# Branch input from scaled streams, bias products between the M products, and accumulating DMAs for the mix, in a four-layer attention and feed-forward kernel

## The reference, cut to what matters

```python
H_res = sinkhorn_log(x_norm @ W_res.T + H_res_base)   # per token 4x4, 50 row and 50 column normalisations
H_pre, H_post = softmax(...), softmax(...)             # per token 4 weights each
H_res = (1.0 - g) * I + g * H_res
x_pre = einsum('btnc,btn->btc', x_streams, H_pre)      # 4 streams of 256 columns -> 256
y = x_pre @ W_branch                                   # 256 x 256
x_mixed = einsum('btij,btjc->btic', H_res, x_streams)  # 16 products of 256 columns for each token
return x_mixed + einsum('btc,btn->btnc', y, H_post)
```

## Time and profile before

| what | value |
|---|---|
| median of 3 runs | 1242.49 us |
| profiled execution, its own time | 1239.2 us |
| its span | 1237.4 us |
| TensorE busy | 1180.8 us (95%) |
| VectorE busy | 798.3 us (65%) |
| ScalarE busy | 475.6 us (38%) |
| GpSimd busy | 101.4 us (8%) |
| mean granted clock of TensorE | 0.982 |

### The profile page before, as it was taken

The page is one execution under the profiler, slowest core; times in us unless marked ns, Lnnn a source line. Parts: engine busy times, 40 slices in busy tenths (PEclk is TensorE's granted clock), DMA queues, the critical chain, the costliest instruction groups (busy, mean ns, idle before and its releaser), DMA issues.

```text
span 1237.4 us, 16474 instructions
## 1 busy us (share of the span) xinstructions
PE 1180.8 (95%) x6458; PEld 588.8 (48%) x6458; DVE 798.3 (65%) x1556; ACT 475.6 (38%) x716; POOL 101.4 (8%) x80
## 2 busy tenths in 40 slices
PE   3989999988999999999999999999999999999998
PEld 2434665553454445454444444444444444444444
DVE  7685898989998246887776767767767652222220
ACT  7784353583235223534434334434343231111110
POOL 4410020025101310020000000000001000000000
PEclk8888899998999999999999999999999999999999
DMA  9630000014103214120121121111110231111310
GB/s 370 210 112 1 2 2 1 1 69 137 34 14 107 64 29 143 68 103 12 57 69 65 38 69 35 67 69 34 68 52 24 66 139 47 46 46 47 118 43 22
DMA packets 26061, 83.57 MB, mean 68 GB/s; under 512 B 3648, under 2 KB 4288, under 8 KB 25984
## 3 DMA queue, kind: packets, MB, share of 16 engines
q1 hardware_dynamic: 25984, 82.53, 19.7%
HBM read 76.22 MB, written 6.29 MB: 67 GB/s over the span
## 4 chain that ended last, share of the span: by engine, by line
PE 80%; DVE 12%; ACT 4%; issue 2%; DMA 1%; ACTq 0%; SPq 0%; DVEq 0%
PE PAIR L2221 31%; PE PAIR L1870 12%; PE PAIR L1871 12%; PE PAIR L1872 12%; DVE LORA L1268 3%; PE PAIR L1935 2%; PE PAIR L2178 1%; PE PAIR L1967 1%; DVE LORA L1267 1%; PE PAIR L2033 1%; DVE LORA L1266 1%; PE PAIR L1952 1%; PE PAIR L2058 1%; PE PAIR L2233 1%; ACT POOL L596 1%
## 5 line engine op out<-in xcount | busy, mean ns | idle before, releaser
L1870 PE MATMUL PAIR<-POOL 128*128 128x512 f16 x688 | 261.9, 381 | 3.9 <-DVE POOL L1349 3.0
L1871 PE MATMUL PAIR<-POOL 128*128 128x512 f16 x688 | 261.6, 380 | 0.0
L1872 PE MATMUL PAIR<-POOL 128*128 128x512 f16 x688 | 261.4, 380 | 0.0
L2221 PE MATMUL PAIR<-XT,POOL 128*128 128x512 f16 (+1 forms) x1056 | 239.0, 379 | 1.0 <-ACT ST L842 1.0
L2221 PEld LDWEIGHTS PAIR<-XT,POOL 128*128 128x128 f16 (+1 forms) x1056 | 102.6, 98 | 120.5 <-issue 2.5
L2221 PE MATMUL PAIR<-X,POOL 128*128 128x512 f16 (+1 forms) x528 | 121.2, 379 | 0.0
L1870 PEld LDWEIGHTS PAIR<-POOL 128*128 128x128 f16 x688 | 67.3, 98 | 84.6 <-issue 5.3
L1872 PEld LDWEIGHTS PAIR<-POOL 128*128 128x128 f16 x688 | 67.4, 98 | 81.9 <-issue 1.1
L1871 PEld LDWEIGHTS PAIR<-POOL 128*128 128x128 f16 x688 | 67.5, 98 | 74.2 <-issue 0.8
L1485 DVE SCALAR_TENSOR_TENSOR STG<-STG,PAIR 128x1024 f32<-128x1024 f32 (+2 forms) x32 | 28.1, 884 | 92.7 <-PE PAIR L2233 89.1
L876 ACT ACTIVATE POOL<-STG 128x1024 f16<-128x1024 f32 (+2 forms) x32 | 25.0, 788 | 145.5 <-DVE STG L1485 145.5
(11 more groups left out here) (280 smaller groups left out, 1656.4 us busy)
## 6 DMA issues: line engine op xcount, KB each, us to landing
STG<-in_gate_w SPq DMA_DIRECT2D x21, 512.0 KB, 3.5
STG<-in_up_w SPq DMA_DIRECT2D x21, 512.0 KB, 4.3
STG<-in_ctx_t SPq DMA_DIRECT2D x16, 512.0 KB, 4.2
STG<-in_ctx SPq DMA_DIRECT2D x16, 512.0 KB, 4.4
STG<-in_down_w SPq DMA_DIRECT2D x16, 512.0 KB, 3.5
POOL<-in_ctx SPq DMA_DIRECT2D x12, 512.0 KB, 11.0
X<-in_x SPq DMA_DIRECT2D x8, 512.0 KB, 9.7
out_t<-X SPq DMA_DIRECT2D x16, 256.0 KB, 2.9
```

The source lines that it names most:

```text
L1870: e.matmul(dst, l_hi, r_hi, start=first, stop=False)
L1871: e.matmul(dst, l_hi, r_lo, start=False, stop=False)
L1872: return e.matmul(dst, l_lo, r_hi, start=False, stop=last)
L2221: i = e.matmul(dst, blk[:, a_, k, :], src[:, b_, k, :], start=(opens and k == 0 and n == 0), stop=(k == KD // 2 - 1 and n == 2), skip_grou ...
```

## The change

- `bias_products` goes. Its matmuls stand inside `m_half`, two of 2 columns after each group of three 512-column matmuls, 256 as before; `bias_raw` (ScalarE) and `bias_terms` (VectorE) move behind M and behind the mix of batch 1. `row_sums` (TensorE) moves ahead of `logit_product(1)` and `row_terms` (VectorE) ahead of the logits.
- The branch input: ScalarE scales the four streams of `H` (`branch_streams`, 4 x 128x256), GpSimd adds them up in three operations of 128x256 (`branch_sum`), and TensorE only transposes the result (2 transposes).
- `add_share` is an accumulating DMA from GpSimd's queue, each after the one before; tile g of batch 1 is issued after `branch_sum(g + 4)`.
- Batch 2's mix: VectorE does streams 0 and 1 of tiles 4 to 7, ScalarE scales streams 2 and 3 into 1024-column buffers (`mix_help(4)` to `(7)`, two pairs of buffers used in turn), and 8 accumulating DMAs add them (`add_help`), one at a time.
- 30 joint Sinkhorn steps and 69 for each batch alone, in portions of 1, 27, 11, 11, 11, 6, 2 where they were 1, 25, 11, 11, 11, 5; `bias_terms` stands between `norm_ask(2, 4)` and `norm_rest(2, 4)`, ahead of the first of them.
- GpSimd's `context_lo` is four operations of 256 columns instead of one of 1024.
- PSUM pairs change: `MIX_PAIR` 3, 1 to 1, 0 and `T3_PAIR` 0, 2, 3, 1 to 2, 3, 1, 0; `third_transpose(0)` waits for the last `m_lo`, `third_transpose(1)` for `braw_ok`.

```diff
-JOINT = 35
+JOINT = 30
@@ GpSimd
+            def branch_sum(g):
+                b_, half = BS[g % 2], D // 2
+                e.wait_ge(bs_ok, g + 1)
...
+                e.tensor_tensor(b_[:, 0:CST], b_[:, 0:CST], b_[:, half:half + CST], ALU.add)
+                e.tensor_tensor(b_[:, CST:half], b_[:, CST:half], b_[:, half + CST:D], ALU.add).then_inc(p_step, 1)
+                e.wait_ge(p_step, 6 + g)
+                e.tensor_tensor(XB[g % 2], b_[:, 0:CST], b_[:, CST:2 * CST], ALU.add).then_inc(bx_ok, 1)
             def add_share(g):
                 e.wait_ge(py_ok, g + 1)
-                e.tensor_tensor(X[:, g, :], X[:, g, :], SHARE[g], ALU.add).then_inc(share_ok, 1)
+                if g:
+                    e.wait_ge(summed, 16 * g)
+                e.dma_start(X[:, g, :], SHARE[g], accum_op=ALU.add).then_inc(summed, 16)
+            def add_help(g):
+                for n in range(2):
+                    e.wait_ge(mixed, g + 1)
+                    e.wait_ge(help_ok, 2 * (g - 2) + n + 1)
+                    e.wait_ge(summed, 16 * (NT + 2 * (g - BT) + n))
+                    e.dma_start(X[:, g, :], XT1M[2 * (g % 2) + n], accum_op=ALU.add).then_inc(summed, 16)
@@ GpSimd, context_lo
-                e.tensor_tensor(lo, STAGE[n % SLOTS], hi, ALU.subtract).then_inc(c_lo, 1)
+                for q in range(0, D, CST):
+                    last = e.tensor_tensor(tile[:, 1, q:q + CST], STAGE[n % SLOTS][:, q:q + CST], tile[:, 0, q:q + CST],
+                                           ALU.subtract)
+                last.then_inc(c_lo, 1)
@@ GpSimd, order
-            for g in range(BT):
-                add_share(g)
+            for g in range(NT):
+                branch_sum(g)
+                if 4 <= g:
+                    add_share(g - 4)
...
+            for g in range(BT, NT):
+                add_help(g)
@@ ScalarE
-                    i = e.activation(DG[g % 2][:, n, :], IDF[:, :], ACT.Copy, scale=PRE[:, NST * g + n:NST * g + n + 1])
+                    i = e.activation(BS[g % 2][:, n * CST:(n + 1) * CST], H[:, g, n * CST:(n + 1) * CST], ACT.Copy,
+                                     scale=PRE[:, NST * g + n:NST * g + n + 1])
@@ ScalarE, mix_help
+                if g >= BT:
+                    e.wait_ge(summed, 16 * (NT + max(0, 2 * (g - BT - 1))))
@@ ScalarE, order
             exponential(0)
+            mix_help(4)
+            mix_help(5)
             weights_hi(0)
             exponential(1)
+            mix_help(6)
+            mix_help(7)
             weights_hi(1)
             exponential(2)
@@ VectorE, order
+            bias_terms()
+            norm_rest(2, 4)
             second_steps(0, 1)
-            norm_rest(2, 4)
             done = 1
-            for n, more in enumerate((25, 11, 11, 11, 5)):
+            for n, more in enumerate((27, 11, 11, 11, 6, 2)):
...
+                elif n == KD // 2:
+                    maximum(0)
@@ TensorE, m_half
                 for d in range(KD):
                     last = m_step(i, d, h)
+                    for s_ in range(2):
+                        bias = e.matmul(PAIR[3][:, at:at + 2], W2[2 * d + h][:, s_, i * P:(i + 1) * P],
+                                        BQ16[:, d, 2 - 2 * h:4 - 2 * h], start=False, stop=(d == KD - 1 and s_ == 1),
+                                        skip_group_check=True)
@@ TensorE, branch_in
-                    for n in range(NST):
-                        at = n * CST + k * P
-                        i = e.matmul(PAIR[3][:, k * P:(k + 1) * P], H[:, g, at:at + P], DG[g % 2][:, n, :],
-                                     start=(n == 0), stop=(n == NST - 1))
+                    i = e.transpose(PAIR[3][:, k * P:(k + 1) * P], XB[g % 2][:, k * P:(k + 1) * P], IDF[:, :])
```

More of the change, by code:

```diff
@@ L289, in build @@
                              "lgt_ok", "lg_raw"))
[L290 to L291 removed]
+        w_hi, m_hi, m_lo, braw_ok, sink_a, soft_a, bs_ok, xp_ok, y_ok, py_ok, help_ok, mdg_ok = (
+            sem(n) for n in ("w_hi", "m_hi", "m_lo", "braw_ok", "sink_a", "soft_a", "bs_ok", "xp_ok", "y_ok",
                              "py_ok", "help_ok", "mdg_ok"))
@@ L997, in _ @@
             m_lo_of(KD - 1)
+            bias_raw()
             third_normal(1)
@@ L1302, in weight_lo, with mix @@
                                        ALU.subtract).then_inc(w_lo, 1)
[L1304 to L1311, removed]
+            def mix(g):
+                sj1 = 1 if 2 <= g < BT else 2
+                e.wait_ge(summed, 16 * (g + 1))
+                for sj in range(sj1):
                     for si in range(NST):
@@ L1315, in mix @@
                                                    xs, ALU.mult, ALU.add)
-                    chain(i)
+                    if g < BT or sj + 1 < sj1:
+                        chain(i)
+                if g >= BT:
+                    i.then_inc(mixed, 1)
             def mix_end(g):
@@ L1669, in _ @@
             mix_factors(1)
-            mix(4, 0, 2)
-            maximum(0)
-            mix(4, 2, 4)
+            mix(4)
             weights_sum(0)
-            stats_of(4)
-            mix(5, 0, 2)
+            mix(5)
+            mix(6)
             maximum(1)
             weights_lo(0)
-            mix(5, 2, 4)
+            mix(7)
+            mixed_stats(4)
             weights_sum(1)
-            stats_of(5)
-            mix(6, 0, 2)
+            mixed_stats(5)
+            weights_lo(1)
             maximum(2)
-            weights_lo(1)
-            mix(6, 2, 4)
             weights_sum(2)
+            mixed_stats(6)
             maximum(3)
@@ L1692, in _ @@
             weights_sum(3)
-            stats_of(6)
-            mix(7)
-            stats_of(7)
+            mixed_stats(7)
             norm_ask(4, 8)
@@ L1987, in m_half @@
                     e.wait_ge(ctx_ok, 1)
+                    e.wait_ge(bq_ok, 1)
+                    e.wait_ge(tmp_ok, 1)
+                    e.wait_ge(lg_raw, B)
+                    e.matmul(PAIR[3][:, HALF + 64:HALF + 65], ONESF[:, :], col(TMP), start=True, stop=True)
                 elif i in (1, 2) and h == 0:
@@ L2038, in branch_product @@
                 e.wait_ge(xp_ok, g + 1)
-                if g:
-                    e.wait_ge(y_ok, g)
-                else:
+                if g == 0:
                     e.wait_ge(wb_in, 16)
                 for k in range(2):
-                    i = e.matmul(PAIR[3][:, HALF:HALF + CST], XPT[g % 2][:, k, :], WBF[:, k, :], start=(k == 0),
+                    i = e.matmul(PAIR[3][:, CST:2 * CST], XPT[g % 2][:, k, :], WBF[:, k, :], start=(k == 0),
                                  stop=(k == 1))
@@ L2064, in third_transpose @@
                 e.wait_ge(n3_ok, g + 1)
-                if g < 2:
-                    e.wait_ge(m_lo, KD - 1 + g)
+                if g == 0:
+                    e.wait_ge(m_lo, KD)
+                elif g == 1:
+                    e.wait_ge(y_ok, NT)
+                    e.wait_ge(braw_ok, 1)
                 if g >= BT:
```

110 lines of the change are left out of this document (48 added, 62 removed).

## The result

The changed kernel takes 1251.28 us (median of 4 runs, 1249.9 to 1251.96), the kernel before 1242.44 on the same chip: ratio 1.0078, 95% interval 1.0059 to 1.0097. It is slower by 0.8%, where 1232.0 was forecast.

What follows compares the result with a forecast made beforehand. TensorE was four fifths of the wait chain, with VectorE's Sinkhorn chain late up to 260 us and at 290 to 333. Gains 5.5 + 9.4 + 0.95 - 5.3 = 10.5 us gave 1228.7, as median 1232.0; range 1224 to 1241.

Steps and rivals of the forecast that it cites:

- quarters of 0.53 us now meet some 22 steps; at 0.25 us each they make VectorE 5.5 us slower there: Projections and score(0): GpSimd's quarters slow VectorE's Sinkhorn steps by 5.5 us, bringing back about 2.2 us of new waits.
- the three waits, 8.6 us, go: Projections, 290 to 321 us: TensorE's three waits for VectorE's lo halves vanish, as batch 2's 28 steps finish earlier.
- Rival 3: Quarters don't help, Sinkhorn scalings lose as much as before: gain about 1 to 3 us, 1240 us; chance 0.13.
- Factors of batch 1: VectorE's Sinkhorn chain beside M: the factors come 5.4 us earlier, at 225.6 instead of 230.9.
- M's end, 226: TensorE's building of M starts near 125.2 and ends near 226 instead of 241.6, saving 15 us.
- rival 4: TensorE's 15 us saved at M come through: gain near 20 us, 1222 us; chance 0.04.
- The first projection, 262.5: Behind the factors of batch 1, all VectorE's: the first projection moves 5.5 us earlier, from 268.0 to 262.5.
- Accumulations, L = 5.2: Batch 2's mix: time from one accumulating DMA's issue to the next is 5.2 us, kept open from 3.5 to 11.
- rival 1: Accumulations are quick, L under 3.9, with no wait on ScalarE: gain 15.9 us, 1226.6 us; chance 0.24.
- rival 2: Accumulations are slow: gain used up at L = 7.0, 1250 us at L = 8, half clock returns; chance 0.12.
- The wait for the third exponential: After score(3), TensorE waits 5.3 us for exponential(2), which follows mix_help(7) and four accumulations on ScalarE.
- The sum: Whole kernel: 5.5 + 9.4 + 0.95 - 5.3 = 10.5 us off the profiled execution.

Runs made afterwards that it cites:

- run 1: Changed kernel with GpSimd's context_lo as one operation of 1024 columns again: 1249.16 us, ratio 1.0061.
- run 4: Changed kernel with context_lo in two operations of 512 columns: 1248.67 us, ratio 1.0061.
- run 5: Changed kernel with GpSimd waiting for the landing of the accumulating DMAs of add_share(6) and add_share(7), quarters back to back: 1244.03 us, ratio 1.0021.
- run 7: Changed kernel with a wait for the first quarter only of context_lo(0) and context_lo(2), behind two DMAs: 1238.12 us, ratio 0.9969.
- run 2: Kernel before with only context_lo changed, to four operations of 256 columns, no DMA issued by GpSimd there: 1238.18 us, ratio 0.9969.
- run 6: Changed kernel with batch 2's four shares added by GpSimd instructions again instead of DMAs: 1247.19 us, ratio 1.0049.
- run 3: Changed kernel with GpSimd waiting for each quarter of context_lo to end before starting the next: 1238.9 us, ratio 0.9975.
- run 11: Run 8 with the 256 bias matmuls in one piece ahead of M instead of between M's products: 1230.66 us, ratio 0.9907.
- run 9: Changed kernel with the edits of run 7 and run 8 together, without waits between all quarters: 1235.25 us, ratio 0.9953.
- run 10: Run 3 with batch 2's mix wholly on VectorE, no add_help and no mix_help(4) to (7): 1235.68 us, ratio 0.9959.
- run 12: Run 8 with 35 joint Sinkhorn steps instead of 30: 1237.05 us, ratio 0.9966.
- run 8: Run 3 with mix_help(7) behind exponential(2) on ScalarE and mixed_stats(4) to (6) later on VectorE, around score(2): 1231.27 us, ratio 0.9922.

## Why the prediction was wrong, by its steps

**The step that failed** is "quarters of 0.53 us now meet some 22 steps; at 0.25 us each they make VectorE 5.5 us slower there", and with it "the three waits, 8.6 us, go". I took from the earlier trace rows that a hold ends with the GpSimd operation that it met. That is true of operations behind a real wait (runs 1, 4, 5, 7) or behind an add (runs 2, 6), and false for those directly behind a DMA that GpSimd issues. The cost was 4.20 + 15.23 us of VectorE, 12.7 us of TensorE's time in one wait, and the lower clock beside it (0.56 from 300 to 312 us). Waits that break the run took 12.4 to 13.2 us off (runs 3 and 7). The forecast named "scalings that last through several quarters" as what would show it wrong, but only as a trace to look for; it stood in no rival's price. Rival 3 has the right place and the wrong size: it counted one hold per operation, so nothing slower than 1240.

The row of the Trainium skill that I leaned on, SBUF — State Buffer, "Who interferes with whom", says that an instruction with two SBUF inputs contends with a GpSimd one that reads SBUF. The scaling has two inputs and the quarters read, so the contention itself agrees. My reading of it ("the new DMAs would cost the Sinkhorn chain nothing") was about the DMA alone; the runs show a cost of the DMA and what is queued behind it together, which no row before could show, since GpSimd issued no DMA there. The same section says that the issue order decides who blocks, not the operation's shape. No run here varies the order of issue; what the runs show is a long hold beside each of three shapes: 8.84, 9.22 and 15.23 us beside operations of 1024, 512 and 256 columns.

**Factors of batch 1**: right. 225.6 forecast, 224.90 measured. Scalings beside `branch_sum` took at most 0.87 us.

**M's end, 226**: 4.5 us too early (230.5). Its own terms give 226.8: M starts 7.2 us earlier, 2.2 of clock and 12.5 of branch input go, 7.1 of bias products come. The bias pairs cost what they should (a pair 0.055 us), the branch products (L2073) waited 1.9 us for ScalarE's copies, and the remaining 1.8 have no single row. It mattered little: TensorE still waited 3.4 us behind M. In run 11 M starts 6.4 us later and the next stage no later, and rival 4 falls with it.

**The first projection, 262.5**: right in run 3 and others (262.60), 3.0 us late in the profiled execution of the changed kernel (265.52). Here are the first diagonal product and its clock, changed kernel, then run 3:

```profile
233.94 8.42 PE L2084 MATMUL PAIR<-POOL,T4B 128*128 128x256 f32 x24 [3.38 <-ACT T4B L765]
...
234.00:242.00 8.00, 8.00 (x24) 0.62 0.00 0
```
```profile
233.98 5.42 PE L2090 MATMUL PAIR<-POOL,T4B 128*128 128x256 f32 x24 [1.76 <-ACT T4B L771]
...
234.00:239.00 5.00, 5.00 (x23) 1.00 0.00 0
```

The forecast expected TensorE idle for 8 us there and did not price the clock behind it. In all profiled executions with the change's front part, idle times of 3.4 to 5.0 us at this place were followed by the lower clock (runs 6, 9, 10, 12 and the changed kernel), those of 1.7 and 1.8 us were not (runs 1, 3, 4, 5, 7, 8). The two go with the clock at M's start, although the code is the same up to there (run 12 aside): changed kernel, then run 3,

```profile
125.00:130.00 5.00, 5.00 (x37) 1.00 0.02 5
...
125.00:130.00 5.00, 5.00 (x24) 0.66 0.02 5
```

At full clock there, as forecast, M ends 1.7 us earlier, TensorE waits longer and the half clock comes behind M instead, where it costs 3.0 us. Why an execution falls on one side is not shown; the edit of run 3 comes into play only later. So the miss of 3.0 us is a cost that I left out, and "right" in run 3 is in part luck. A saving on TensorE ahead of a wait can cost more than it gives.

**Accumulations, L = 5.2**: right. Two issues of batch 2's mix, as for the earlier trace rows:

```profile
344.20 0.88 POOL L532 DMA_DIRECT2D X<-XT  x1 [37.23 <-DVE X L1350]
349.41 0.86 POOL L532 DMA_DIRECT2D X<-XT  x1 [4.33 <-DMA X<-XT]
```

Periods of 5.1 to 5.5 us here (5.1 to 6.1 for batch 2's shares). Rivals 1 and 2 fall: L was neither under 3.9 nor over 7. The wait for the third exponential, 5.8 us where 5.3 was forecast, is right in size but not step by step. `mix_help(7)` started at 364.70, four periods behind mix(4) as worked out, and took 3.3 us, not 4.1. Then `exponential(2)` did not follow `weights_hi(1)` at once: ScalarE waited 2.88 us for `maximum(2)`, which stands on VectorE behind `weights_lo(1)`, and that waited for `weights_hi(1)`. `mixed_stats(5)`, in the same queue, had waited 6.48 us for a DMA before (to 364.62). The forecast had no term for this way through VectorE.

**The sum.** With the hold taken away (run 3) the changed kernel gains 2.5 us over the kernel beside it, with the order of run 8 9.6 us. The forecast of 10.5 had counted the wait at the exponential as a loss of 5.3 already, so even run 3 is 8 us short of it. In its trace the waits for the projection's lo halves are gone altogether, 2.2 us better than forecast, and that for the exponential is 0.3 longer. Two things stood in no term. TensorE waits 4.3 us for the context's lo halves (0.9 in the kernel before), 3.4 more. And behind these two waits the clock is down, where the kernel before kept it up. First the kernel before, then run 3:

```profile
345.00:380.00 35.00, 34.13 (x170) 1.00 0.27 87
...
355.00:360.00 5.00, 5.00 (x17) 0.50 0.52 99
...
370.00:375.00 5.00, 2.78 (x8) 0.60 0.73 256
375.00:380.00 5.00, 5.00 (x22) 0.72 0.02 7
```

From these rows I estimate 2.5 + 1.1 + 1.4 = 5.0 us. Together 3.4 + 5.0 + 0.3 - 2.2 = 6.5 of the 8 us; the rest stays open. The forecast had the half clock only in rival 2, behind "a long idle"; waits of 5.6 and 3.9 us were enough.

## What to carry to other kernels

Where GpSimd issues a DMA and computes behind it, let it wait for the end of its first operation there: here that was worth 13 us. Before counting a saving on an engine, look for the last-arriving input of the stage behind it, and price an idle time of a few us on TensorE with the clock that follows it (in run 3 an estimated 5.0 us behind waits of 5.6 and 3.9). An instruction that waits for a slow chain (a statistic, a help product) belongs behind everything that others wait for and that is ready: that order alone gave some 7 us.

The best versions beat both kernels: quarters with waits and the other order, 1231.27 us, and the same with the bias products ahead of M, 1230.66.

## What the runs showed of the hardware

- VectorE's scaling of two SBUF inputs (128x64, 0.23 us alone) is held by GpSimd operations: one operation long (2.19 us at 1024 columns, 0.67 on average in a run of quarters, 1.58 at most in run 9) where none stands unbroken behind a DMA issue; through the whole queued run (8.84, 9.22 and 15.23 us) where one does. Waits that are already met, as the one on `c_hi` in front of each `context_lo`, did not break it (24 quarters in one piece of 15.57 us); a wait on the quarter just issued or on the DMA did. Whether a DMA that does not accumulate does the same was not tried, and why the issue has this effect stays open.
- An accumulating DMA of 512 KB within SBUF: issue 0.86 us on GpSimd, landing 4.6 us (median of 16), one after the other every 5.1 to 5.5 us in batch 2's mix and 5.1 to 6.1 us for its shares.
- GpSimd's add of 128x1024 takes 2.35 us, the quarter of `context_lo` 0.63 us back to back (15.14 / 24) and 0.74 with waits between (17.69 / 24): a wait costs GpSimd 0.1 us.
